# Winograd rows in seven image pairs instead of five, their preparation moved to VectorE, away rows moved to ScalarE and GpSimd

## The reference

```
def _gn(v, G=32, eps=1e-05):          # mean and variance over 2 channels x 56 x 56
    g = v.reshape(B_, G, C_ // G, H_, W_)
    ...
    return ((g - m) / jnp.sqrt(s + eps)).reshape(v.shape)
bw = cw + jax.lax.stop_gradient(jnp.sign(W) - cw)          # the signs of W
x = x + conv_general_dilated(_gn(x), bw, window_strides=(1, 1), padding=((1, 1), (1, 1)), ...)
```

## Time and profile before

| | |
|---|---|
| median of three runs | 201.56 us |
| span of the profiled execution | 200.7 us |
| around its span (median less span) | 0.9 us |
| PE busy | 191.2 us, 95% |
| DVE busy | 165.3 us, 82% |
| POOL busy | 166.7 us, 83% |
| ACT busy | 149.7 us, 75% |

### The profile page before, as it was taken

One profiled execution on the slowest core, in us unless ns is written; L12 is line 12 of the kernel. 1 busy time (PEld: TensorE's weight loads), 2 busy tenths in 40 slices (PEclk: granted clock), 3 DMA queues, 4 the chain that ended last, 5 costly groups with the idle time before them and its releaser, 6 DMA issues.

```text
span 200.7 us, 10042 instructions
## 1 busy us (share of the span) xinstructions
PE 191.2 (95%) x4482; PEld 168.4 (84%) x4482; DVE 165.3 (82%) x363; ACT 149.7 (75%) x142; POOL 166.7 (83%) x85
## 2 busy tenths in 40 slices
PE   1999999999999999999999999999999999999990
PEld 0478888879858988988999988899998999889990
DVE  2799999996999997799988779998779999627392
ACT  3185999799989289899909989972998999595000
POOL 1029786999999999999999997999999899999500
PEclk9999999999999999999999999999999999999999
DMA  6978977871787988868697887868887883906274
GB/s 216 362 217 292 331 246 252 289 209 44 306 243 291 297 316 282 282 248 278 242 301 296 275 327 276 325 228 321 326 241 296 266 319 152 381 13 238 116 283 175
DMA packets 18698, 52.17 MB, mean 260 GB/s; under 512 B 2080, under 2 KB 5024, under 8 KB 18656
## 3 DMA queue, kind: packets, MB, share of 16 engines
q1 hardware_dynamic: 18656, 51.54, 72.9%
HBM read 25.84 MB, written 25.69 MB: 257 GB/s over the span
## 4 chain that ended last, share of the span: by engine, by line
PE 65%; ACT 14%; DVE 13%; DMA 3%; issue 1%; SPq 0%; DVEq 0%; ACTq 0%
PE psum L738 65%; ACT halves L424 5%; DVE stats L500 5%; ACT xnorm L418 4%; DMA xbuf<-in_x_dram 3%; ACT moved L437 3%; DVE xbuf L570 2%; DVE xbuf L556 1%; DVE xbuf L580 1%; DVE own L508 1%; ACT line_halves L447 1%; ACT std L413 1%; DVE xbuf L544 1%; ACT lines_norm L451 1%; DVE halves L538 1%
## 5 line engine op out<-in xcount | busy, mean ns | idle before, releaser
L738 PE MATMUL psum<-halves,w_taps 64*64 64x385 f16 (+8 forms) x4140 | 183.4, 325 | 0.5 <-DVE halves L532 0.4
L738 PEld LDWEIGHTS psum<-halves,w_taps 64*64 64x64 f16 x4140 | 156.7, 107 | 19.3 <-ACT moved L437 0.9
L330 POOL TENSOR_TENSOR halves<-xnorm,halves 128x784 f16<-128x784 f32 (+5 forms) x35 | 91.6, 2637 | 20.0 <-ACT xnorm L418 19.7
L500 DVE BATCH_NORM_STATS2 stats<-xbuf 128x6 f32<-128x448 f32 x112 | 60.8, 613 | 4.3 <-DMA xbuf<-in_x_dram 4.1
L424 ACT ACTIVATE halves<-xbuf,coef 128x784 f16<-128x784 f32 (+5 forms) x35 | 50.7, 1449 | 3.0 <-DVE coef L525 2.8
L418 ACT ACTIVATE xnorm<-xbuf,coef 128x784 f32<-128x784 f32 (+5 forms) x35 | 50.5, 1443 | 0.0
L437 ACT ACTIVATE moved<-psum 64x784 f32<-64x784 f32 (+1 forms) x30 | 25.5, 850 | 7.9 <-PE psum L738 7.3
L345 POOL TENSOR_TENSOR xbuf<-xbuf,moved 128x784 f32<-128x784 f32 (+1 forms) x15 | 29.3, 1956 | 0.4 <-ACT moved L437 0.4
L570 DVE SCALAR_TENSOR_TENSOR xbuf<-psum,xbuf 64x784 f32<-64x784 f32 (+1 forms) x32 | 28.2, 881 | 1.0
L556 DVE SCALAR_TENSOR_TENSOR xbuf<-psum,xbuf 128x784 f32<-128x784 f32 x21 | 20.3, 967 | 7.6 <-PE psum L738 7.4
L371 POOL TENSOR_TENSOR line_halves<-lines_norm,line_halves 128x1512 f16<-128x1512 f32 (+1 forms) x10 | 20.9, 2120 | 0.5 <-ACT lines_norm L451 0.5
(11 more groups left out here) (36 smaller groups left out, 72.0 us busy)
## 6 DMA issues: line engine op xcount, KB each, us to landing
xbuf<-in_x_dram SPq DMA_DIRECT2D x48, 448.0 KB, 4.6
out_dram<-xbuf SPq DMA_DIRECT2D x43, 392.0 KB, 4.0
xbuf<-in_x_dram SPq DMA_DIRECT2D x16, 224.0 KB, 4.1
out_dram<-xbuf SPq DMA_DIRECT2D x5, 504.0 KB, 3.9
out_dram<-xbuf SPq DMA_DIRECT2D x5, 448.0 KB, 3.8
out_dram<-xbuf SPq DMA_DIRECT2D x5, 364.0 KB, 4.1
out_dram<-xbuf SPq DMA_DIRECT2D x5, 252.0 KB, 4.1
out_dram<-xbuf SPq DMA_DIRECT2D x1, 224.0 KB, 3.8
```

Source lines behind the costliest of these rows:

```text
L330: nc.gpsimd.tensor_tensor(at(halves[:, k % HRING, 1, :], a, b), at(xnorm[:, k % NRING, :], a, b), at(halves[:, k % HRING, 0, :], a, b), AL ...
L500: nc.vector.bn_stats(stats[:, n, :], xbuf[:, s, n * STAT:(n + 1) * STAT]).then_inc(blocks_ready, 1)
L738: mm = pe.matmul(outs[:, :, left:right], weights, ins[:, :, left + dx:right + dx], start=first_step, stop=last_step)
```

## The change

The list `WINOGRAD` grows from 3, 6, 9, 12, 14 to 3, 6, 8, 10, 12, 14, 15; the last pair gets product units and other small blocks. `lines` and `line_halves` have two buffers, `lines_norm` is gone. ScalarE rounds all the lines in one instruction; VectorE makes the sum (`sum_line`) and the lower halves (`lo_lines`), each in one instruction with two tensors of SBUF as inputs. ScalarE and GpSimd take the away units of all pairs but the last, except the five in `BY_VECTOR`. A first away unit is moved and added between the two chunks of the next pair when that is plain, and after them when it is a product pair. VectorE's statistics are split around the additions, and the third coefficient (L525 before) is made for product pairs alone, in `aggregate`.

```diff
-WINOGRAD = (3, 6, 9, 12, 14)
+WINOGRAD = (3, 6, 8, 10, 12, 14, 15)
+
+BY_VECTOR = {(0, 0), (1, 0), (3, 1), (6, 1), (14, 1)}
...
         if k == LAST:
-            return [[(0, 7), (14, 7)], [(28, 7), (42, 4)], [(50, 3)]]
+            return [[(WROW + WROWS, 7)], [2, 1], [0, 3], [(WROW + WROWS + 7, 3)], [(WROW + WROWS + 10, 3)]]
...
         if k == LAST:
-            return [[(7, 7), (21, 7)], [(35, 7), (46, 4)], [(53, 3)]]
+            return [[(0, 8), (8, 8)], [(16, 6)], [(22, 3)]]
...
-        return k != LAST and i == (0 if k in WINOGRAD else 1)
+        return k != LAST and (k, i) not in BY_VECTOR
...
-        lines = sb("lines", [128, 4 * WN], F32)
-        line_halves = sb("line_halves", [128, 2, 4 * WN], F16)
-        lines_norm = sb("lines_norm", [128, 4 * WN], F32)
+        lines = sb("lines", [128, 2, 4 * WN], F32)
+        line_halves = sb("line_halves", [128, 2, 2, 4 * WN], F16)
...
             def store_unit(k, i):
+                if k == LAST:
+                    wait_away(k, 0)
+                    store(k, 0, 0, 16)
+                    sp.wait_ge(home_done, home_before(k) + 3)
+                    store(k, 1, WROW, WROW + WROWS + 7)
...
-                nc.gpsimd.tensor_tensor(lines[:, SUM].rearrange("p (r w) -> p r w", w=W), odd, even,
-                                        ALU.add).then_inc(lines_made, 1)
-
-            def lo_lines(k):
...
             for k in range(NP):
 
-                if k >= 2 and k - 2 not in WINOGRAD and k != WINOGRAD[0]:
+                if k >= 2 and by_scalar(k - 2, 1):
                     add_away(k - 2, 1)
-                for c in range(len(chunks(k))):
+                last = len(chunks(k)) - 1
+                for c in range(last):
                     if (k, c) != (0, 0):
                         lo(k, c)
...
+                if k in WINOGRAD:
+                    lo(k, last)
+                if k >= 1 and by_scalar(k - 1, 0):
+                    add_away(k - 1, 0)
+                if k not in WINOGRAD:
+                    lo(k, last)
...
                 if k + 1 in WINOGRAD:
                     make_lines(k + 1)
-                if k in WINOGRAD:
-                    lo_lines(k)
-                if k - 1 in WINOGRAD:
-                    add_away(k - 1, 0)
...
+                act.wait_ge(lines_made, 2 * n + 2)
+                act.wait_ge(sum_made, n + 1)
...
+                nc.scalar.activation(line_halves[:, n % 2, 0, :], lines[:, n % 2, :], ACT.Identity,
+                                     scale=coef[:, k % XRING, 0:1]).then_inc(line_hi_ready, 1)
...
                 if k in WINOGRAD:
+                    hi(k, last)
+                    normalise(k, last)
+                if k >= 1 and by_scalar(k - 1, 0):
+                    move_away(k - 1, 0)
+                if k not in WINOGRAD:
+                    hi(k, last)
+                    normalise(k, last)
+                if k in WINOGRAD:
                     line_upper(k)
                 if k + 1 < NP:
                     deviation(k + 1)
-                if k - 1 in WINOGRAD:
-                    move_away(k - 1, 0)
...
+            def sum_line(k):
...
+                nc.vector.scalar_tensor_tensor(lines[:, n % 2, SUM].rearrange("p (r w) -> p r w", w=W),
+                                               pairs_of_rows[:, :, 0:W], coef[:, s, 2:3], pairs_of_rows[:, :, W:],
+                                               ALU.add, ALU.add).then_inc(sum_made, 1)
+
+            def lo_lines(k):
+                n = winograd_before(k)
+                dve.wait_ge(line_hi_ready, n + 1)
...
+                nc.vector.scalar_tensor_tensor(line_halves[:, n % 2, 1, :], lines[:, n % 2, :], coef[:, k % XRING, 0:1],
+                                               line_halves[:, n % 2, 0, :], ALU.mult, ALU.subtract).then_inc(line_lo_ready, 1)
...
+                if k >= 1:
+                    if k - 1 in WINOGRAD:
+                        add_outer(k - 1)
+                    else:
+                        add_home(k - 1, 1)
+                    if not by_scalar(k - 1, 1):
+                        add_away(k - 1, 1)
+                if k in WINOGRAD:
+                    lo_lines(k)
+                if k + 1 in WINOGRAD:
+                    sum_line(k + 1)
...
+            add_away(LAST, 0)
+            add_outer(LAST)
+            add_home(LAST, 3)
+            add_away(LAST, 1)
+            add_home(LAST, 4)
+            add_away(LAST, 2)
```

More of the change, by code:

```diff
@@ L125, in aways_before, with last_product @@
     def aways_before(u):
-        return sum(0 if by_scalar(k, i) else len(away_units(k)[i]) if k == LAST and i else 1 for k, i in AWAY[:u])
+        return sum(not by_scalar(k, i) for k, i in AWAY[:u])
     def winograd_before(k):
         return sum(p < k for p in WINOGRAD)
+    def last_product(k):
+        return home_blocks_before(k, 3)
     def chunks(k):
@@ L307, in _ @@
                 store_unit(k, 0)
[L308 to L312, removed]
             for k in range(NP - XRING, NP):
@@ L550, in add_home @@
                 if k in WINOGRAD:
-                    (first, rows), (second, fewer) = home_units(k)[i]
-                    add_rows(k, bank, first, rows)
-                    add_rows(k, bank + 1, second, fewer).then_inc(home_done, 1)
+                    *begun, (j, (first, rows)) = enumerate(home_units(k)[i])
+                    for before, (first_before, rows_before) in begun:
+                        add_rows(k, bank + before, first_before, rows_before)
+                    add_rows(k, bank + j, first, rows).then_inc(home_done, 1)
                     return
@@ L562, in add_away @@
                 dve.wait_ge(away_conv, away_blocks_before(k, i + 1))
+                unit = away_units(k)[i]
+                size = unit[0][1] * W
                 if k in WINOGRAD:
-                    first, rows = away_units(k)[i][0]
-                    part, made = at(xbuf[:, k % XRING, :], first, first + rows), psum[:, bank, 0:rows * W]
+                    first = unit[0][0]
+                    part = xbuf[:, k % XRING, first * W:first * W + len(unit) * size].rearrange("p (n m) -> p n m", m=size)
                 else:
                     part = at(xbuf[:, k % XRING, :], 28 * i, 28 * i + 28).rearrange("p (n m) -> p n m", m=2 * BN)[:, :, BN:]
-                    made = psum[:, bank:bank + 2, 0:BN]
+                made = psum[:, bank:bank + len(unit), 0:size]
                 for here, there in ((LOW, HIGH), (HIGH, LOW)):
                     nc.vector.scalar_tensor_tensor(part[here], made[there], 1.0 / SCALE,
-                                                   part[here], ALU.mult, ALU.add).then_inc(away_done, 1)
-            def add_last(n, home, away):
-                dve.wait_ge(home_conv, home_blocks_before(LAST, 1) + n + 1)
-                add_rows(LAST, home.bank, home.first, home.rows).then_inc(home_done, 1)
-                dve.wait_ge(away_conv, away_blocks_before(LAST, 1) + n + 1)
-                part = at(xbuf[:, LAST % XRING, :], away.first, away.first + away.rows)
-                for here, there in ((LOW, HIGH), (HIGH, LOW)):
-                    nc.vector.scalar_tensor_tensor(part[here], psum[there, away.bank, 0:away.rows * W], 1.0 / SCALE,
                                                    part[here], ALU.mult, ALU.add).then_inc(away_done, 1)
@@ L692, in wait_upper @@
                     pe.wait_ge(products_ready, 3)
-                    pe.wait_ge(line_hi_ready, 2 * winograd_before(k) + (2 if b.product == 1 else 1))
+                    pe.wait_ge(line_hi_ready, winograd_before(k) + 1)
             def wait_lower(b):
```

118 lines of the change are left out of this document (58 added, 60 removed).

## The result

| | before | after |
|---|---|---|
| median of the runs | 201.66 us (4) | 212.19 us (4; 211.77 to 213.52) |
| ratio | 1 | 1.0519 (1.048 to 1.0559) |
| span of the profiled execution | 200.7 us | 210.2 us |

The kernel became 10.5 us slower. The forecast was 204.0 us, its range ended at 209.0: the sign was right, the time was 3.2 us outside. What happened is the rival "exclusion at the port" (VectorE's passes with two SBUF inputs and GpSimd's instructions stand still for each other). I had it at 209.1 us, 206 to 211, with a chance of 0.28, and its price was too low.

The account below looks back on a forecast made before the run. TensorE, 95% busy, was taken to bound the kernel. Pair 15's start at 184.3 plus 15.15 to VectorE's end gave 199.45, plus 3.6 a span of 203.1, plus 0.9 outside it 204.0 us; range 200.9 to 209.0.

Parts of the forecast that it names:

- exclusion at the port: VectorE's two-input passes and GpSimd block each other, in middle and last pair: 209.1 us (206 to 211), chance 0.28.
- the forecast's mechanism: GpSimd's late chunks stall TensorE at pairs 10, 12, 14 (+2.6 us); VectorE's late lower halves make the last pair cost 1.9.
- Part 1: What is removed on TensorE: columns, a hiccup and a small start-up instruction, so pair 15 would start at 181.75 us.
- One more product pair, -1.29: TensorE before the last pair: one more pair costs a product pair's time instead of a plain one's, saving 1.29 us.
- Hiccup, -0.6: TensorE's four waits on ScalarE's away-row copy go, as pair 3's unit is copied before pair 4's second chunk: -0.6 us.
- Two more product pairs on VectorE, 2 x 3.1: VectorE's added busy time for two more product pairs, six additions of 0.63 replacing one of 0.97: 3.1 us each.
- Part 2: The middle, pairs 8 to 14: GpSimd's work fits but in the wrong order; three stalls, +2.6 us, pair 15 at 184.3.
- Stalls of 0.86 at pairs 10, 12 and 14, none at 8: TensorE waits 0.86 us for GpSimd's second-chunk lower halves at three pairs; at pair 8 GpSimd is 0.36 in time.
- VectorE and ScalarE hidden: In the middle, both engines' changed work was counted as costing no time, VectorE being about 172 us busy.
- Loads behind stores at nothing: SP's loads queue behind stores awaiting GpSimd's additions, but have three pairs to land: no cost, at most 0.9 us.
- Part 3: The last pair: VectorE's late lower halves and a later bank wait end it 15.15 us after its start, costing 1.9 more.
- The pass at 2.25: VectorE's lower halves of the lines (128x2016) in the last pair take 2.25 us, bounds 1.7 to 2.5.

Follow-up runs that it names:

- e1: Changed kernel, VectorE's sum and lower halves replaced by statistics with one SBUF input, their values left out: 203.62 us, ratio 1.0065.
- e4: Changed kernel with one-input passes (values left out), last pair plain, and second away units of pairs 8, 10, 12 on VectorE: 200.34 us, ratio 0.99.
- c4: Kernel before the change, with pair 3's first away unit copied and added ahead of pair 4's second chunk: 202.26 us, ratio 1.0002.
- e5: Changed kernel, only the sum of the lines reading one SBUF tensor (value left out), lower halves still two: ratio 1.0313, 208.6 us by the ratio.
- c2: Changed kernel, last pair plain, second away units of pairs 8, 10, 12 on VectorE, two-input passes, all values computed: 208.8 us, ratio 1.0312.
- e3: Changed kernel with both VectorE passes reading one SBUF input (values left out) and the last pair plain: 202.41 us, ratio 1.0017.
- e6: Changed kernel, lower halves made by one-input statistics in the last pair alone, sums and other pairs unchanged: 209.33 us, ratio 1.0333 to 1.0416.

## Why the prediction was wrong, step by step

**Where 10.5 us come from.** By experiments: the exclusion 8.6 us (212.19 to e1's 203.62; by the ratios 1.0519 and 1.0065, each to the runs of before beside it, 9.2). By the traces of these two, 2.45 of them are lost before pair 15 starts (186.13 against 183.68) and 5.97 in it (20.03 against 14.06): 3.7 of longer waits and 2.2 of clock. The other 2 us (1.3 by e1's ratio) are the forecast's mechanism: the middle stalls 2.1, the last pair 1.2, less what one more product pair gives.

**Part 1.** *One more product pair, -1.29*: right; 10.51 against 11.82 wherever nothing is late, and e4 has pair 15 at 181.48 where I had 181.75. *Hiccup, -0.6*: gone in e1 (10.52 and 11.82), but in the changed kernel pair 4 takes 12.03, and alone (c4) it is worth nothing measurable: the four waits were read as a gain, though the sum of a wait is not what its removal brings. *Two more product pairs on VectorE, 2 x 3.1*: by its own terms 6 x 0.63 - 0.97 = 2.8 each, a slip of 0.6 us of busy time that changes nothing else.

**Part 2.** *Stalls of 0.86 at pairs 10, 12 and 14, none at 8*: the mechanism was right, place and count too; by itself each is 0.68 to 0.74 (e1), and e4 removes them by removing the addition I had named. With the port they are 1.35, 1.36 and 1.13, where the rival had 1.7, and 0.38 at pair 8 where it had 0.3. *VectorE and ScalarE hidden*: right without the port; with it VectorE's lateness decides in e5 and c2. *Loads behind stores at nothing*: e4 shows no wait on them.

**Part 3.** *The pass at 2.25*: 2.1 by itself. *Lower lines at 5.2, chunk at 2.5, the wait before the last home unit at 1.5, VectorE's end at 15.15*: 5.38, 2.60, 1.30 and 15.09 in e1. The nearness is in part luck: the statistics take 2.44 where the pass takes 2.1, and TensorE's weight loads waited 1.4 us for the chunk and then 0.8 for the lines, where I had the one inside the other. The products of the last pair cost 1.2 us without the exclusion (e1 against e3). *Even in time, no gain*: not shown, since in no run both were in time. *Tail 3.6*: 3.0 (207.19 to 210.2).

**Sum.** Without the exclusion the forecast's 204.0 stands against 203.62. That is in part luck, since two errors cancel in it: the span came to 201.8, not 203.1, and outside the span lie 1.8 us in all these executions (212.04 against 210.2, e1's 203.63 against 201.8), not 0.9. Before's 200.7 belongs to an execution slower than its median of 201.56, which less 1.8 is 199.8; its spans in the runs go from 199.4 to 201.2. Only a profiled execution's own time makes that term.

**The step that failed** is the paragraph on the port: "no row of before bears on it", so the chance stayed at 0.28, the sum had the port at nothing, and the range ended at 209.0, below this rival's own 209.1. True for the rows, but GpSimd's additions and subtractions all have two inputs in SBUF and it runs 83% of the span; a pass of VectorE that needs the same port must meet it. The runs show 8.6 us for what the sum had at nothing. And the rival's size was wrong where it mattered. I gave the last pair +2.3, as if the delays of a meeting were used up within the pair in which it falls. Behind pair 13's second chunk GpSimd has no wait left in which to make good, not even in e1: what it lost in pair 14's meeting it carried into pair 15 (e6), met the next pass there, and TensorE's single long wait then cost it the clock.

## What to carry to other kernels

Count the SBUF inputs of each VectorE instruction before moving one beside a busy GpSimd: here one pass of 2.1 us took 2.0 us from GpSimd and lost up to 4.7 itself, with no idle time in any row. When an instruction gets longer at the same shape, look at what the other engine ran in that moment, and test by an instruction of the same length with one input, which costs one run. A delay is over only when the engine next idles: follow it to that row, and where it ends as one long wait of TensorE, add the clock.

## What the runs showed of the hardware

- A waiting VectorE pass got the port after one of GpSimd's instructions in the changed kernel (3.80 us for 2.1), after three in e5 (6.83, in one execution), with GpSimd's instructions back to back in both. The Trainium skill (SBUF — State Buffer, Summary: rules for kernel authors) says that the second to issue blocks until the first finishes; e5 shows a longer wait, and the measurement decides.
- An edit can change its sign with the exclusion: three away units on VectorE gained 2.1 us without it and cost 3.6 with it.
- Without matmuls for 5.8 us TensorE came back at a granted clock of 0.54; after a wait of 3.8 us in e6's profiled execution it stayed at 1.0. In e6's other three runs its mean was 0.992, and they have no rows.
